# A dense-slot mixture-of-experts block around a Mamba mixer: one wait fewer for the second of each pair of gathers and scatters

## The reference, cut to what matters

```python
def _moe(x, Wr, br, W1, b1, W2, b2):                  # E = 8 experts, H = 512, D = 128, TOP_K = 2
    logits = xt @ Wr + br
    top_vals, top_idx = jax.lax.top_k(logits, TOP_K)
    gate = softmax over the two chosen logits
    h = relu(einsum('td,edh->teh', xt, W1) + b1)
    y = einsum('teh,ehd->ted', h, W2) + b2
    return einsum('ted,te->td', y, gate)

x = L0_attn_x                                          # (4, 512, 128) float32, 2048 tokens
x = x + 0.5 * moe(layernorm(x))
x = x + mamba_block(layernorm(x))                      # projection, causal conv, state scan, gating, projection, norm
x = x + 0.5 * moe(layernorm(x))
```

## Time and profile before

| | us |
|---|---|
| runs of the kernel | 408.42, 411.36, 411.74 (median 411.36) |
| the profiled execution, its own time | 408.86 |
| its span, from the first to the last instruction | 407.1 |
| POOL busy, of the span | 222.4 (55%) |
| PE busy, of the span | 331.2 (81%) |
| DVE busy, of the span | 270.2 (66%) |
| ACT busy, of the span | 209.7 (52%) |

### The profile page before, as it was taken

One profiled execution on the slowest core, in us unless ns is written; L12 is line 12 of the kernel. 1 busy time (PEld: TensorE's weight loads), 2 busy tenths in 40 slices (PEclk: granted clock), 3 DMA queues, 4 the chain that ended last, 5 costly groups with the idle time before them and its releaser, 6 DMA issues. The chain is left out here.

```text
span 407.1 us, 8915 instructions
## 1 busy us (share of the span) xinstructions
PE 331.2 (81%) x2366; PEld 295.5 (73%) x2366; DVE 270.2 (66%) x920; ACT 209.7 (52%) x501; POOL 222.4 (55%) x263
## 2 busy tenths in 40 slices
PE   7996999999970688899999999777499999999000
PEld 7885899989970666577777779777489989998000
DVE  4884677656740479687888986898567766665026
ACT  3743566656740355637567583544256666775002
POOL 4016555565666285463756879660655555665712
PEclk9988999999995598899999999668899999999755
DMA  6791111111111500000000000011111111111154
GB/s 162 216 315 45 42 37 42 41 45 42 40 44 49 206 1 2 0 0 2 1 2 3 0 0 2 2 52 53 40 40 39 42 41 40 41 40 40 45 194 134
DMA packets 18674, 22.23 MB, mean 55 GB/s; under 512 B 4114, under 2 KB 13508, under 8 KB 18628
## 3 DMA queue, kind: packets, MB, share of 16 engines
q1 hardware_dynamic: 13092, 11.18, 9.1%
q0 software_dynamic: 4096, 8.40, 6.9%
q10 hardware_dynamic: 1440, 2.11, 1.4%
HBM read 14.33 MB, written 7.34 MB: 53 GB/s over the span
## 5 line engine op out<-in xcount | busy, mean ns | idle before, releaser
L482 POOL DMA_INDIRECT XG<-xn_rows,rows_in x64 | 61.9, 967 | 79.7 <-DMA XG<-xn_rows,rows_in 32.3
L798 PE MATMUL PS<-XT_all,W1B 128*128 x624 | 87.6, 284 | 8.8 <-DVE XT_all L1459 8.7
L798 PEld LDWEIGHTS PS<-XT_all,W1B 128*128 128x128 f32 x624 | 77.7, 196 | 12.3 <-issue 11.1
L494 POOL DMA_INDIRECT y_rows<-YS,rows_out x64 | 64.0, 1000 | 37.1 <-DMA y_rows<-YS,rows_out 27.7
L810 PE MATMUL PS<-H,W2B 128*128 128x128 f32 x624 | 83.3, 277 | 0.0
L1126 ACT ACTIVATE H<-PS,W1B 128x128 f32<-128x128 f32 x156 | 48.9, 364 | 58.0 <-PE PS L798 57.0
L810 PEld LDWEIGHTS PS<-H,W2B 128*128 128x128 f32 x624 | 76.4, 193 | 0.3
L1489 DVE COPY W2B<-W2S 128x513 f32 x78 | 35.3, 452 | 39.0 <-DVE YT_all L1480 35.0
L1116 ACT ACTIVATE W1B<-W1S 128x516 f32 x78 | 49.4, 633 | 21.4 <-DMA W2S<-in_L_ffn_W 7.6
L655 PE MATMUL PS<-ones 128*128 128x128 f32 x236 | 40.8, 350 | 17.2 <-DMA YT_all<-y_rows 16.2
L655 PEld LDWEIGHTS PS<-ones 128*128 128x128 f32 x236 | 39.6, 264 | 18.5 <-DMA YT_all<-y_rows 16.4
(11 more groups left out here) (204 smaller groups left out, 558.4 us busy)
## 6 DMA issues: line engine op xcount, KB each, us to landing
YT_all<-y_rows SPq DMA_DIRECT2D x8, 512.0 KB, 5.6
W1S<-in_L_ffn_W SPq DMA_DIRECT2D x1, 2048.0 KB, 11.1
W2S<-in_L_ffn_W SPq DMA_DIRECT2D x8, 256.0 KB, 8.3
xn_rows<-XN ACTq DMA_DIRECT2D x8, 256.0 KB, 4.3
X<-in_L_attn_x SPq DMA_DIRECT2D x4, 256.0 KB, 4.9
XG<-xn_rows,rows_in POOLq DMA_INDIRECT x64, 2.5
y_rows<-YS,rows_out POOLq DMA_INDIRECT x64, 2.2
out_x<-X SPq DMA_DIRECT2D x4, 256.0 KB, 2.3
```

Of the source, the lines that this page charges most:

```text
L482: g.indirect_dma_start(out=XG[:, u, :], out_offset=None, in_=xn_dram, in_offset=bass.IndirectOffsetOnAxis(ap=rows_in[:, i:i + 1], axis=0), ...
L494: g.indirect_dma_start(out=y_dram, in_=YS[:, u, :], in_offset=None, out_offset=bass.IndirectOffsetOnAxis(ap=rows_out[:, i:i + 1], axis=0), ...
L798: last = mm(PS[2 + 2 * half + j % 2][:, c * P:(c + 1) * P], W1B[w][:, h * P:(h + 1) * P], XT_all[:, ds(start, P)], start=True, stop=True)
```

## The change

For gathers from the ninth on, the wait for `s_xt` stays only where the freed tile begins a new group: at gathers 8 to 14 and then at 16, 18 ... 30. Gathers 15, 17, 19 ... 31, nine in each layer, keep only the wait for `s_issued`. The second condition gets the upper bound `i < XG_RING`, so that those nine don't fall through to the wait for `s_rows`. For scatters, the wait for `s_ysc` stays at the first tile of each group only; scatters 3, 7, 11 and 15 of each layer lose it.

```diff
@@ -472,10 +472,10 @@
                 for i in range(DENSE):
                     u = i % XG_RING
-                    if i >= XG_RING:
+                    if i == XG_RING or (i > XG_RING and (GROUP_OF[i - XG_RING] != GROUP_OF[i - XG_RING - 1])):
 
                         pool.wait_ge(s_xt, layer * len(ARRIVALS) + GROUP_OF[i - XG_RING] + 1)
-                    elif i == 0 or i >= FIRST_ROW:
+                    elif i == 0 or FIRST_ROW <= i < XG_RING:
 
                         pool.wait_ge(s_rows, layer + 1)
                     transfer_written()
@@ -487,7 +487,7 @@
                 for m, tiles in enumerate(LEAVES):
                     for i in tiles:
                         u = i % YS_RING
-                        if i == tiles[0] or (m % 2 and i < DENSE // 2):
+                        if i == tiles[0]:
 
                             pool.wait_ge(s_ysc, layer * len(LEAVES) + m + 1)
                         transfer_written(len(tiles) > 1)
```

## The result

The kernel with the change took 427.25 us (median of 4 runs, 419.78 to 430.26); the kernel before 411.55 (4 runs, 408.42 to 414.02; three of them are the runs of the table under "Time and profile before", the fourth is 414.02). The ratio is 1.029, 95% interval 1.023 to 1.036: **slower by 2.9%**, where 398.5 us, with a range of 395.2 to 402.0, was forecast. Run again unchanged, the same kernel took 392.42 us in one set of runs (ratio 0.968) and 418.93 in another (1.033). So there are two things to explain: what the change does to the waits, and what sometimes turns the gain into a loss.

The account below looks back on a forecast made before the run. GpSimd's queue of 32 gathers, then 32 scatters, was taken to bound each expert stage. Nine gathers at 0.44 us and four scatters at 0.46 give 5.8 us per stage; 410.1 - 11.6 = 398.5 us, range 395.2 to 402.0.

Parts of the forecast that it names:

- The price of a second wait, and the sum: GpSimd's expert-stage queue: 0.44 us per gather, 0.46 per scatter, 5.8 us per stage, 11.6 us in all.
- So nothing takes GpSimd's place: after this change it is still the last one.: End of expert stages: ScalarE's copies keep at least 3.6 us spare before the last scatter, so GpSimd stays the bound.
- Rival (1), TensorE or ScalarE becomes the release: Gathers: eight buffers too few, transpose waits bind; only the scatters' 3.7 us stay, 406.4 us; chance 0.03.
- The ring of eight: Gather buffers: gather i needs the buffer of gather i-8, freed by TensorE's transposes; tightest at gather 18.
- 1.2 us to spare at gather 18: First expert stage: transposes of tiles 10 and 11 end early enough to leave gather 18 this spare time.
- Rival (2): GpSimd's indirect DMAs: the wait isn't what costs; only 26 x 0.017 us go, 409.7 us; chance 0.02.
- Rival (3): Closer descriptor writing on GpSimd collides with VectorE's copies: slower, up to 414.5 us; chance 0.03.
- means above 1.06 us: Indirect DMAs in the profile after: mean durations above this would speak for collisions with VectorE's copies.
- the rule that was weighed there: VectorE's SBUF copies block GpSimd's descriptor writing: gathers could wait 0.43 us each; trace shows at most about 0.2.
- Between the stages: Mixer stage starts 5.8 us earlier, TensorE's idle shrinks from 16.2 to about 11.4 us; clock effect taken as 0.
- The clock: TensorE's clock falls in the idle and returns as before; bounds 0 and 3 us, taken as 0.
- GpSimd's irregularities: Extra idle at gather 19, first stage, and scatter 17, second stage: -1.4 to +1.4 us, taken as 0.

Follow-up runs that it names:

- again: The changed kernel, unedited, run again beside the kernel before: 392.42 us, ratio 0.968.
- before2: The kernel before, unchanged, profiled beside a repeat of the changed one: 406.76 us, ratio 1.000.
- four: The kernel before with the wait taken from gathers 25, 27, 29 and 31 of each stage alone: 402.11 us, ratio 0.990.
- again2: The changed kernel, unedited, run once more in another set beside the kernel before: 418.93 us, ratio 1.033.
- extra2: The kernel before plus one DMA of 128 rows of 4 bytes on SP's queue behind each gather, second run: 416.79 us, ratio 1.025.
- few: The kernel before plus one DMA of 16 rows of 4 bytes on SP's queue behind each gather: 415.91 us, ratio 1.024.
- gathers3: The kernel before with only the gathers' part of the change, third run: 413.25 us, ratio 1.013.
- half2: The kernel before with only the gathers changed, each bringing 64 of 128 numbers per row, second run: 411.04 us, ratio 1.014.
- extra: The kernel before plus one DMA of 128 rows of 4 bytes on SP's queue behind each gather, first run: 404.41 us, ratio 0.996.
- pace: The kernel before with only the gathers changed, plus a GpSimd memset ahead of each pair's first gather from gather 16: 396.29 us, ratio 0.977.

## Why the prediction was wrong, point by point

- **The price of a second wait, and the sum.** 0.44 and 0.46 us each were right: the earlier trace rows have them, the changed kernel shows 0.30 us of idle at all the edited places, and 65 separate semaphore instructions as said. Without late signals the change gained 13.4 us, not 11.6. The parts measured 9.4 and 4.9 us where 7.9 and 3.7 had been summed. The surplus is at least partly in the scatters: of the 61 distances between neighbours other than the one at scatter 17 of layer 1, ten in the profile of before are 0.1 to 0.25 us over the 1.27 or 1.73 of their kind, 1.75 us in all, and three in *again*, 0.3 us in all; I had counted none of these. So 392.4 us lay below the range too, by 2.8 us. Most of that is the starting point and not the sum: the forecast began at 410.1 us, the mean of four times of before, and before took 405.8 beside *again*. From 405.8 the same sum gives 394.2.
- **"So nothing takes GpSimd's place: after this change it is still the last one."** This is the step that failed. It rested on at least 3.6 us that would be left between ScalarE's last copy and the last scatter, read from one profile. In the profile of *again* 2.6 us are left and it held. In the recorded result the copies came 19.6 us later than in rows 6, because TensorE's signals reached VectorE and ScalarE up to 5.6 us after its matmuls' ends, and that path set the end of both stages. The sum had no term for this, and no row of before has such a signal. The kernel before was itself affected in such a set (*before2*) and hid it in the 9 us by which its GpSimd queue was the longer.
- **Rival (1), TensorE or ScalarE becomes the release**, named the right releaser but with the wrong cause and bound: it kept the scatters' 3.7 us. The ring of eight hardly bound without late signals, but its 1.2 us to spare at gather 18 were gone. In *again* (PE, then POOL, layer 0) the transposes of tiles 10 and 11 end at 55.77 us, 1.05 later than in rows 3, and gather 18 is put down to them with 0.94 us of idle, 0.2 over the rule:

```profile
55.39 0.38 PE L783 MATMUL PS<-ident,XG 128*128 128x128 f32 x2
```

```profile
56.04 0.95 POOL L482 DMA_INDIRECT XG<-xn_rows,rows_in  x1 [0.94 <-PE PS L783]
```

- **Rival (2)** fell with *again*. **Rival (3)**, longer descriptor writing beside VectorE's copies, was the only one on the right side of zero, and its own sign, means above 1.06 us, did not appear: the means are 956 and 995 ns (967 and 1000 before), the medians 946 and 972 as before. The trace does not show the rule that was weighed there (the Trainium skill, SBUF — State Buffer, section "SBUF: two separate sides") at a size that matters here.
- **Between the stages.** From the fillers' start to the first gather of layer 1 it took 148.9 us in the profile of before, 146.2 in *again*, 146.1 in the changed kernel. But it was 145.6 in *before2* and 148.3 in *four*: over all the profiles it lies either between 145.6 and 146.8 or between 148.0 and 148.9, whatever the kernel. So the profile of before was a long one, and its difference to *again* must not be put down to the change; whether the two pairs of times of before belong to these two groups was not tried. The clock fell in the idle and came back as forecast. Windows over the idle and the 17 us behind it, of *again* (us, busy us of PE, PEld, DVE, ACT, POOL, granted clock, DMA share, GB/s):

```profile
119.90:128.60 8.70, 0.00 (x0) 0.00 (x0) 0.00 (x0) 0.00 (x0) 2.91 (x3) 0.70 0.40 125
128.70:145.70 17.00, 15.77 (x91) 13.13 (x92) 14.23 (x55) 10.59 (x29) 11.34 (x13) 0.86 0.18 73
```

A mean of 0.86 behind the idle stands beside the 0.82 of the earlier trace rows. The first normalised rows come at 135.36 us, 6.7 behind the fillers' start, against 144.03 - 136.35 = 7.7:

```profile
135.36 1.11 DVE L1343 TENSOR_SCALAR XN<-X,mv,rs 128x128 f32<-128x128 f32 x4 [0.48 <-POOL rs L506]
```

- **GpSimd's irregularities.** Scatter 17 of layer 1 stands 2.64 us behind its neighbour in every profile (2.71 in *again2*), so the extra 1.4 us stayed. They were priced right, at 0.

What is shown: the removed waits cost 0.44 us each; where TensorE's signals are late, the path through TensorE and no longer GpSimd's queue sets the end of both stages, and the gain turns into the loss; within the sets that have them, their number in the gather phase rises when gathers stand closer or small DMAs are added. What is open: why some sets have them and others not. Chip 11 showed both kinds, the kernel before takes nearly the same time in both (405.3 to 405.8 us without, 405.6 to 406.6 with late signals, but 411.55 in the recorded result, whose changed kernel also took 8.3 us more than *again2*), and every profile with late signals also has fewer semaphore records (3,493 to 3,836 of them, against 4,948 to 5,948 in the others). The two could have one cause, and it can't be excluded that recording the execution is part of it. Open as well is whether the mean pace or the closeness within a pair decides; the run for it fell into a set without late signals.

## What to carry to other kernels

Dropping a second wait from a GpSimd indirect DMA is worth 0.44 us for each, if GpSimd's queue sets the end. But measure such a change in more than one set of runs: with its gathers one every 1.47 us instead of 1.69, this kernel ran at 392 us in one set and at 419 and 427 in two others, while the kernel before held 405 to 412 in all. And read slack as a buffer: the 9 us by which the queue of before was longer than the path through TensorE looked like waste, and in *before2* they were what kept its time the same in spite of the late signals.

## What the runs showed of the hardware that had not been expected

- TensorE's signals can reach other engines up to 6.5 us late (*extra2*). In the recorded result seven of them arrive in a burst, 0.04 to 0.09 us apart, while signals of DMAs and of ScalarE come on time in between. In such a set more of them came when small DMAs were added (*extra2*, *few*) or gathers moved closer (*gathers3*); half the bytes in each gather made no difference outside the intervals (*half2*).
- Sixteen rows of 4 bytes behind each gather, 64 such DMAs in all on another engine's queue, cost 10.4 us by the medians (*few*, runs between 410.0 and 420.1 us) in a set with late signals; 64 DMAs of 128 such rows cost nothing, 1.1 us less than before, in a set without them (*extra*).
- The idle of 0.75 us before an indirect DMA with two waits takes in a memset of 0.33 us for nothing (*pace*), so GpSimd can do short work there.
